# Own order tables for three of four batches, reordered gathers and a rearranged start in a Mamba plus mixture-of-experts kernel

## The chip, the cores and the metric

The kernel runs on one core of a Trainium2 chip. The time is the device time of one execution in microseconds, as the median of several runs. For the kernel before it is 1083.17 us (three runs, 1080.89 to 1084.44).

## The reference

Four sequences of 512 tokens with 512 channels. First a selective scan (Mamba) over a context of 256 channels, gated by the layer-normed x and added to it; then a mixture of 64 experts with the top 6 per token, and a shared expert.

```python
# b = 0..3, L = 512, d_model 256, d_inner 512, d_state 16, dt_rank 16
x1 = einsum('bld,ed->bel', ctx, in_proj_w)
u  = silu(causal_conv4(x1, conv_w) + conv_b)
dt_low, Bm, Cm = split(einsum('bdl,ed->bel', u, x_proj_w), [16, 32], axis=1)
dt = softplus(einsum('brl,dr->bdl', dt_low, dt_proj_w) + dt_proj_b)
A  = -exp(A_log)
state = state * exp(dt * A) + (dt * u) * B      # scan over the 512 steps
y  = sum_n(state * C) + D * u
x  = x + swapaxes(y * silu(layernorm(x)), 1, 2)
h  = layernorm(x)
# 64 experts, hidden 352, top 6 of softmax(h @ gate_w.T), capacity 64 per expert
x  = x + combine(w_down(silu(w_gate h) * w_up h)) + silu(h @ sw_gate) * (h @ sw_up) @ sw_down
```

## The kernel before

All matrices are float32. The work has two phases.

**First phase.** Each of the four batches b has 32 scan steps q (`STEPS`): four blocks of 128 inner channels, times eight pairs of states. A step takes 2 x 512 columns and five operations: `dA` (ScalarE, L918, exp(dt A) into PSUM), `dbu` (GpSimd, L1341, dt u B), `scan` (VectorE, L1105), `weigh` (times C; VectorE at L1112 for odd steps and those in `EXTRA`, GpSimd at L1346 for the others), and `yT` (TensorE, L566, eight transposes that accumulate y in PSUM). The product buffer `R` is a ring of five, so dbu of step q + 5 waits for yT of step q (L1340). `gate` (L1128) and `x2` (L1133) multiply by silu(z) and add x.

Before the scans of a batch stand its preparation: transposes of the context (`ctx`), the projection (`inproj`, L597), the first tap (`acc`, L858), three more taps (`conv`, L1119), `u` (silu), `xdbl` (L605), and, for each block, dt by softplus. The stable softplus is made of ScalarE's exp and ln and four GpSimd operations of 512 columns, `c`, `sp`, `dt` and `dtu` (L1314, L1319, L1323, L1334). After the scans come the layer norm (`xstats` L1155, `xaggr` L1094, `xn` L951, `xnT`), the router (`logits`, `top`, `choose`, `pos`, `places`, `hots`, `ohsid`, `table`) that builds the table of token numbers per expert, and the shared expert of the batch: `sgate` and `sup` (L696, 24 matmuls each, which the trace records as two matmuls apiece), `sdown` (L709, 24 matmuls) and VectorE's addition (L1144). For batch 3 the shared expert's `sup` and `sdown` are done in the second phase.

What each engine does next is fixed by hand-written times. `AT` gives, for each engine and kind of work, the time in steps counted from a batch's first scan, so that 64 + 64.1 for `sdown` of batch 2 is step 128.1, after the last scan; `LAST` overrides it for batch 3. `first_phase` (L339) sorts all of it, and each engine takes its own entries in this order (`mine`). The times decide the order only; semaphores decide when a thing starts. An engine that waits for one entry holds all that are behind it. `BANKS` says which PSUM bank an entry takes.

```python
"dve xstats": [35.07, 35.57, 36.07, 36.23],              # AT
"pe sdown": [64.1, 64.41, 64.47, 65.75, ..., 68.44],     # AT
"dve sdown": [65.41, 67.2, 68.24, 69.79],                # AT
"dve xstats": [34.49, 35.55, 36.17, 36.55],              # LAST, on top of 96
```

**The start.** SyncE issues the context, nine parameter loads that count on one semaphore, then x, zeros and shared weights (L459 to L481). TensorE waits for all nine (L575), transposes all parameters (L576 to L581), waits for their copies (L582), and only then takes its first entry. The buffers of step 0 are cleared and A is made by exp and a sign change.

**Second phase.** 32 pairs q of experts. The weights come in 192 pieces of 704 or 768 KB through 20 slots (`PIECES`, `SLOTS`); the first 20 are fetched around the last scans, each further one when its slot is free (L543). For a pair, GpSimd gathers 128 token rows by an indirect DMA (`gather`, L1355), TensorE transposes them (`tokens`) and does gate and up (`gate_up_mm`, L733), `acts`, `down_mm` (L757) one pair later, and `merge` (L765), which sums rows of a token that is in both experts; GpSimd adds the rows to the output by an indirect DMA (`scatter`, L1365). Each scatter, and each of the four additions of the shared expert of batch 3 (`add_shared`, L1373), waits for the one before it. There are two buffers for gathered rows (`xg`): gather q waits for tokens q - 2 and for VectorE's `weights` q - 2 (L1353). The items of batch 3's shared expert are spread over pairs 0 to 27 (`items`). The orders of the engines around this are:

```python
tokens(0)                                   # TensorE, L792
for q in range(NPAIR):
    if q + 1 < NPAIR: tokens(q + 1)
    gate_up_mm(q)
    if q: down_mm(q - 1)
    acts(q); merge(q - 1); shared items
for q in range(3): gather(q)                # GpSimd, L1381
for q in range(NPAIR):
    if q + 3 < NPAIR: gather(q + 3)
    add_shared items; scatter(q)
```

## Time and profile before

| | |
|---|---|
| median of the runs | 1083.17 us (1080.89 to 1084.44) |
| profiled execution, its own time | 1084.39 us |
| span of the profiled execution | 1082.5 us |
| mean granted TensorE clock | 0.893 |
| busy: TensorE, VectorE, ScalarE, GpSimd | 892.9, 597.4, 503.0, 572.7 us |
| moved by DMA | 250.50 MB, mean 231 GB/s |

The profile is of one execution, taken by the hardware's profiler. PE is TensorE's matmul, PEld its weight load, DVE VectorE, ACT ScalarE, POOL GpSimd, SPq SyncE's queue. L566 is line 566 of the kernel. Times are microseconds from the start of the span. A row of the timeline gives start, duration, engine, line and operation, what it writes and reads, how many instructions it groups (x), and in brackets for how long the engine had been idle and what released it. A row by windows has the busy time of each engine in that stretch with the number of instructions. An engine can be busy and still not be what is waited for.

### The profile page before, as it was taken

What the parts mean: (1) busy time and instruction counts of PE and PEld (TensorE: products, weight loads), DVE (VectorE), ACT (ScalarE), POOL (GpSimd) and SP (SyncE); (2) the same over time, 40 slices, a digit from 0 to 9 for tenths busy, and PEclk for the clock granted to TensorE, in tenths of its full rate; (3) what the DMA queues carried; (4) which work ended last, traced back from release to release, by engine and by line L of the source; (5) the groups of instructions that cost most, each with busy time, mean ns of one, the idle gap of its engine ahead of it and who ended that gap; (6) DMA issues with size and microseconds to landing.
All of it is one profiled execution on the core that took longest, in us unless ns stands there. A gap on an engine that the chain in (4) does not pass through costs nothing.

```text
span 1082.5 us, 12258 instructions
## 1 busy us (share of the span) xinstructions
PE 892.9 (82%) x4049; PEld 482.9 (45%) x4049; DVE 597.4 (55%) x849; ACT 503.0 (46%) x871; POOL 572.7 (53%) x326
## 2 busy tenths in 40 slices
PE   5346745769899778998769998999999899979966
PEld 3144434546454465454645553444444444434432
DVE  2279879998888988898898722212211122111111
ACT  3667653887776778665856333121221112111111
POOL 0398899986988868978877301121122112122211
PEclk9768765588999987999789998999999999998988
DMA  9423434434333434334457391999999999999972
GB/s 330 155 80 115 140 134 145 148 116 161 108 129 134 158 134 146 117 118 145 166 202 260 121 354 38 369 398 395 394 399 398 392 394 400 387 390 399 390 269 30
DMA packets 68361, 250.50 MB, mean 231 GB/s; under 512 B 10522, under 2 KB 13094, under 8 KB 68044
## 3 DMA queue, kind: packets, MB, share of 16 engines
q1 hardware_dynamic: 56332, 226.14, 55.0%
q0 software_dynamic: 7744, 18.88, 7.2%
q10 hardware_dynamic: 4224, 4.72, 1.3%
q8 instruction: 33, 0.54, 0.2%
q14 instruction: 28, 0.23, 0.1%
HBM read 230.54 MB, written 19.17 MB: 231 GB/s over the span
## 4 chain that ended last, share of the span: by engine, by line
PE 53%; DMA 15%; DVE 11%; issue 8%; ACT 6%; POOL 5%; SPq 0%; POOLq 0%; DVEq 0%; ACTq 0%
PE ps L696 12%; PE ps L566 11%; PE ps L733 10%; PE ps L709 6%; DMA out_rows<-xn,idxs 5%; DMA arena<-xn_rows,idu 5%; PE ps L757 5%; DVE ps L1105 4%; DVE arena L1112 3%; PE ps L777 2%; PE ps L765 2%; ACT ps L918 2%; PE ps L597 2%; DMA out_rows<-arena 2%; DMA out_rows<-so_or_scores 2%
## 5 line engine op out<-in xcount | busy, mean ns | idle before, releaser
L566 PE MATMUL ps<-ident,arena 128*128 128x128 f32 (+2 forms) x1408 | 240.6, 326 | 127.5 <-POOL arena L1346 48.1
L1341 POOL TENSOR_TENSOR arena<-arena 128x1024 f32<-128x1024 f32 x128 | 299.8, 2359 | 22.2 <-PE ps L566 12.3
L566 PEld LDWEIGHTS ps<-ident,arena 128*128 128x128 f32 (+2 forms) x1408 | 205.9, 180 | 229.5 <-issue 80.3
L918 ACT ACTIVATE ps<-arena,An 128x511 f32<-128x511 f32 x256 | 165.6, 680 | 104.8 <-DVE ps L1113 79.0
L1105 DVE TENSOR_TENSOR_SCAN ps<-ps,arena 128x1024 f32<-128x1024 f32 x84 | 192.1, 2287 | 19.1 <-POOL arena L1341 9.7
L1365 POOL DMA_INDIRECT out_rows<-xn,idxs x32 | 50.9, 1592 | 278.1 <-ACT xn L817 148.5
L733 PE MATMUL ps<-arena 128*64 128x352 f32 x968 | 165.7, 479 | 0.0
L696 PE MATMUL ps<-xnT,sw 128*128 128x512 f32 (+1 forms) x328 | 154.2, 614 | 3.5 <-ACT arena L881 2.7
L1346 POOL TENSOR_TENSOR arena<-arena 128x1024 f32<-128x1024 f32 x44 | 103.7, 2357 | 53.8 <-DVE arena L1105 53.5
L1245 DVE TENSOR_TENSOR arena<-arena,ps 128x352 f32<-128x352 f32 x32 | 16.7, 521 | 207.5 <-PE ps L733 207.5
L1105 DVE TENSOR_TENSOR_SCAN arena<-ps,arena 128x1024 f32<-128x1024 f32 x44 | 100.4, 2282 | 25.3 <-POOL arena L1341 22.9
L733 PEld LDWEIGHTS ps<-arena 128*64 128x64 f32 x968 | 72.8, 142 | 69.9 <-issue 66.7
L1112 DVE TENSOR_TENSOR arena<-ps,arena 128x1024 f32<-128x1024 f32 x84 | 102.6, 1221 | 2.2
L817 ACT COPY routes<-ps 128x512 f32<-128x512 f32 x32 | 18.7, 585 | 168.2 <-PE ps L745 168.2
L696 PEld LDWEIGHTS ps<-xnT,sw 128*128 128x128 f32 (+1 forms) x328 | 58.4, 189 | 70.2 <-issue 65.5
L757 PE MATMUL ps<-arena,routes 118*64 118x512 f32 (+1 forms) x366 | 88.0, 592 | 0.0
L817 ACT COPY arena<-ps 128x512 f32<-128x512 f32 x60 | 35.0, 585 | 72.7 <-PE ps L566 62.9
L709 PE MATMUL ps<-sw,hs 128*128 128x512 f32 x144 | 67.6, 606 | 0.0
L1252 DVE TENSOR_SCALAR routes<-ps,wcol 128x512 f32<-128x512 f32 x32 | 24.0, 751 | 64.1 <-PE ps L757 64.1
L1355 POOL DMA_INDIRECT arena<-xn_rows,idu x32 | 34.3, 1072 | 34.6 <-DVE idu L1226 10.7
L597 PE MATMUL ps<-arena 128*128 128x512 f32 x64 | 37.2, 722 | 12.8 <-DVE arena L1119 10.8
L1022 ACT ACTIVATE arena<-ps 128x352 f32<-128x352 f32 x32 | 14.8, 464 | 67.7 <-PE ps L733 65.8
(151 smaller groups left out, 942.7 us busy)
## 6 DMA issues: line engine op xcount, KB each, us to landing
arena<-bc_rows SPq DMA_DIRECT2D x128, 512.0 KB, 4.7
arena<-in_L_ffn_w_down SPq DMA_DIRECT2D x60, 768.0 KB, 19.7
arena<-in_L_ffn_w_gate SPq DMA_DIRECT2D x61, 704.0 KB, 20.8
arena<-in_L_ffn_w_up SPq DMA_DIRECT2D x60, 704.0 KB, 16.9
arena<-in_x SPq DMA_DIRECT2D x4, 1024.0 KB, 7.0
xn_rows<-xn ACTq DMA_DIRECT2D x4, 1024.0 KB, 4.3
out_rows<-arena SPq DMA_DIRECT2D x4, 1024.0 KB, 5.0
extra<-in_L_ffn_w_up SPq DMA_DIRECT2D x4, 704.0 KB
```

The lines of the kernel that those rows point to most:

```text
L566: return nc.tensor.matmul(dst, src, ident[0:k, 0:k], is_transpose=True, **kw)
L597: mm = nc.tensor.matmul(ps[:, bank, :], winT[:, m, c * P:(c + 1) * P], ctxT[:, m, :], start=(m == 0), stop=(m == 1))
L696: mm = nc.tensor.matmul(ps[0:m, bank, :], w[:, k, c * P:c * P + m], xnT[:, k, :], start=(k == 0), stop=(k == HC - 1))
L709: mm = nc.tensor.matmul(ps[:, bank, :], hs[0:m, k, c * P:(c + 1) * P], swd[0:m, k, :], start=(k == 0), stop=(k == NI - 1))
L733: mm = nc.tensor.matmul(ps[64 * e:64 * e + 64, 2 + n, 0:I], xgT[q % 2][:, k, 64 * e:64 * e + 64], place(what, q, e)[:, k, :], start=(k == ...
L757: mm = nc.tensor.matmul(ps[64 * e:64 * e + 64, 6 + j, :], hT[j][0:m, k, 64 * e:64 * e + 64], place("down", q, e)[0:m, k, :], start=(k == 0 ...
L817: nc.scalar.copy(dst, src).then_inc(sm, 1)
L918: a = nc.scalar.activation(ps[:, 2 * (c % 2) + n, 1:L], dt[k][:, 1:L], ACT.Exp, scale=An[:, k, NB * g + n:NB * g + n + 1])
L1105: V.tensor_tensor_scan(pair if by_vector(q) else flat(R[q % RING]), pair, flat(R[q % RING]), 0.0, ALU.mult, ALU.add).then_inc(s["scan_done ...
L1112: link(V.tensor_tensor(R[q % RING], ps[:, h:h + 2, :], Crep[n % REPS], ALU.mult))
L1341: G.tensor_tensor(R[c % RING], dtu[k][:, None, :].to_broadcast([P, NB, L]), Brep[n % REPS], ALU.mult)\
L1346: G.tensor_tensor(R[c % RING], R[c % RING], Crep[n % REPS], ALU.mult).then_inc(s["cs_even"], 1)
```

## The change

1. Order tables of their own: `FIRST` for batch 0 and `LATE` for batch 2, beside `AT` (batch 1) and `LAST` (batch 3). Many entries of `AT` and `LAST` shift. `EXTRA` now counts steps over all batches: 8, 3, 4 and 5 even steps of batches 0 to 3 are weighed by VectorE, where it was 5 of each.
2. `c`, `sp`, `dt` and `dtu` of blocks 0 and 1 of batch 0 are done by VectorE (`BYV`).
3. Seven parameter loads go to ScalarE's queue; SyncE issues the context, in_proj_w and gate_w, and waits for all before the large loads. TensorE transposes the identity 14 times (`WARM`), then the context and in_proj_w; VectorE copies in_proj_w; the other parameters are transposed after the second projection matmul group.
4. In batch 3 the second half of `ohsid` (token numbers times the one-hot rows) is done by VectorE.
5. Second phase: `gate_up_mm(q)` goes in front of `tokens(q + 1)`, `silu(q)` in front of `evac_tokens(q + 1)`, and four gathers lead, so that gather q + 4 stands in front of scatter q.

```diff
 AT = {
-    "dve zstats": [-4.93, -4.46, -2.23, -1.03],
+    "dve zstats": [-7.68, -7.21, -4.93, -3.78],
-    "pe sup": [58.22, 58.56, 58.62, 59.14, 59.31, 59.34, 59.41, 60.5, 60.64, 61.24, 61.54, 62.15],
+    "pe sup": [58.66, 59.02, 59.08, 59.6, 59.77, 59.8, 59.87, 60.96, 61.1, 61.7, 62.0, 62.61],
-    "pe sdown": [64.1, 64.41, 64.47, 65.75, 66.2, 66.65, 67.47, 67.69, 67.91, 67.99, 68.14, 68.44],
+    "pe sdown": [64.14, 64.45, 64.51, 64.97, 66.24, 66.69, 67.51, 67.73, 67.95, 68.03, 68.18, 68.48],
...
+FIRST = {
+    "pe ctx": [-28.2, -26.8],
+    "act du": [-11.16, -11.01, 4.51, 5.26],
+    "pool c": [-13.61, -10.93, 2.64, 4.09],
+    "pool sp": [-13.31, -10.76, 3.28, 4.67],
+    "pool dt": [-12.79, -10.73, 3.3, 4.91],
+    "pool dtu": [-11.7, -9.33, 5.24, 5.65],
+    "dve zaggr": [3.72],
...
+LATE = {
+    "dve xstats": [35.07, 35.57, 36.07, 36.3],
+    "act xn": [36.8, 37.2, 37.6, 38.0],
+    "pe xnT": [37.1, 37.7, 38.3, 38.9],
+    "pe sgate": [42.01, 42.51, 43.6, 43.9, 45.87, 46.16, 48.36, 48.52, 48.74, 49.03, 49.41, 49.7],
+    "pe sup": [49.85, 50.25, 50.64, 51.05, 51.27, 51.44, 51.84, 52.24, 52.64, 53.03, 53.99, 54.24],
+    "pe sdown": [56.07, 56.46, 56.86, 57.31, 57.72, 58.1, 58.54, 58.94, 59.35, 59.79, 60.18, 60.58],
+    "dve sdown": [57.55, 58.8, 60.04, 61.27],
...
+FIRSTBANKS = {
+    "ctx": [6, 7],
+    "inproj": [4, 5, 6, 7],
+}
...
 LASTBANKS = {
-    "sgate": [0, 1, 0, 1, 0],
+    "sgate": [0, 1, 0, 3, 0],
-    "sel": [1],
+    "sel": [7],
...
-EXTRA = [4, 6, 12, 22, 24]
+EXTRA = [0, 4, 6, 12, 18, 20, 24, 26, 36, 44, 52, 76, 84, 88, 90, 100, 108, 116, 118, 120]
...
+        def sums_by(b, c):
+            return "dve" if b == 0 and c < BYV else "pool"
+
         def by_vector(q):
-            return q % 2 == 1 or q % STEPS in EXTRA
+            return q % 2 == 1 or q in EXTRA
...
+                    own, own_banks = {0: (FIRST, FIRSTBANKS), B - 2: (LATE, LATEBANKS), B - 1: (LAST, LASTBANKS)}\
+                        .get(b, (AT, BANKS))
...
+        def softplus_sum(engine, E, kind, b, c):
+            i = DC * b + c
+            if i == BYV:
+                engine.wait_ge(s[{"c": "c_ready", "sp": "sum_add", "dt": "dt_ready", "dtu": "dtu_ready"}[kind]], i)
+            if kind == "c":
+                engine.wait_ge(s["wm_ready"], i + 1)
+                E.tensor_tensor(rest[c % 2], ex[c % 2], rest[c % 2], ALU.subtract).then_inc(s["c_ready"], 1)
...
             load(cin, ctx_1024[0].rearrange("(t p) d -> p t d", p=P), s["ctx_in"])
-            load(raw_win, in_proj_w.rearrange("(c p) d -> p c d", p=P), s["par_in"])
+            load(raw_win, in_proj_w.rearrange("(c p) d -> p c d", p=P), s["win_in"])
             load(raw_gw, gate_w, s["par_in"])
+            sp.wait_ge(s["win_in"], 16)
+            sp.wait_ge(s["par_in"], 16 * 8)
...
-            pe.wait_ge(s["par_in"], 16 * 9)
...
-            pe.wait_ge(s["pre_ev"], 6)
+            for n in range(WARM):
+                transpose(ps[:, 5, 0:P], ident[:], start=True, stop=True)
+            def flip_parameters():
+                pe.wait_ge(s["par_in"], 16 * 8)
+                flip(1, 0, [raw_vec]).then_inc(s["pre_t"], 1)
+                flip(3, 0, [raw_xp[:, c * P:(c + 1) * P] for c in range(DC)]).then_inc(s["pre_t"], 1)
+                flip(0, 0, [raw_dtw[:, c, :] for c in range(DC)]).then_inc(s["pre_t"], 1)
+                flip(2, 0, [raw_gw[:, c::HC] for c in range(HC)]).then_inc(s["pre_t"], 1)
...
                     flip(bank, 0, [cin[:, t, c * P:(c + 1) * P] for t in range(LT)]).then_inc(s["ctxT_mm"], 1)
+                    if b == 0 and c == 1:
+                        pe.wait_ge(s["win_in"], 16)
+                        for m in range(2):
+                            flip(m, 0, [raw_win[:, k, m * P:(m + 1) * P] for k in range(DC)]).then_inc(s["pre_t"], 1)
...
                     mm.then_inc(s["inproj_mm"], 1)
+                    if b == 0 and c == 1:
+                        flip_parameters()
...
             for q in range(NPAIR):
+                gate_up_mm(q)
                 if q + 1 < NPAIR:
                     tokens(q + 1)
-                gate_up_mm(q)
...
+            load(raw_xp, x_proj_w, s["par_in"])
...
+                    if i == 0:
+                        act.wait_ge(s["par_in"], 16 * 8)
+                        nc.scalar.activation(An[:], An[:], ACT.Exp).then_inc(s["a_exp"], 1)
+                        nc.scalar.preload_act_table_set("silu_and_others")
+                        act.wait_ge(s["pre_t"], 3)
+                        copy(vec[:], ps[:, 1, 0:3 * DC], s["pre_ev"])
...
-                        nc.scalar.activation(ohsid[:, i % 2, :, n, :], ohs[:, c], ACT.Copy, scale=f)\
-                            .then_inc(s["ohsid_ready"], 1)
+                        if n == 0 or b < B - 1:
+                            nc.scalar.activation(ohsid[:, i % 2, :, n, :], ohs[:, c], ACT.Copy, scale=f)\
+                                .then_inc(s["ohsid_ready"], 1)
...
             for q in range(NPAIR):
+                silu(q)
                 if q + 1 < NPAIR:
                     evac_tokens(q + 1)
-                silu(q)
...
+            for m in range(2):
+                dve.wait_ge(s["pre_t"], m + 1)
+                V.tensor_copy(winT[:, m, :], ps[:, m, :]).then_inc(s["win_ready"], 1)
...
+                elif kind == "ohsid":
+                    dve.wait_ge(s["ohs_ready"], i + 1)
+                    if c >= 2:
+                        dve.wait_ge(s["tab_mm"], i - 1)
+                    with nc.allow_low_precision("whole numbers up to 16, exact"):
+                        V.tensor_scalar(ohsid[:, i % 2, :, 1, :], ohs[:, c], float(i + 1), None, ALU.mult)\
+                            .then_inc(s["ohsid2_ready"], 1)
...
-            for q in range(3):
+            for q in range(4):
                 gather(q)
             for q in range(NPAIR):
-                if q + 3 < NPAIR:
-                    gather(q + 3)
+                if q + 4 < NPAIR:
+                    gather(q + 4)
```

## Rows read from the trace of the kernel before

**Rows 1.** Windows by batch: length; PE, PEld, DVE, ACT, POOL busy; clock, DMA, GB/s

```profile
56.00:187.00 131.00, 74.01 (x315) 55.75 (x316) 113.18 (x99) 79.34 (x125) 122.01 (x61) 0.68 0.37 124
187.00:330.00 143.00, 120.18 (x515) 73.75 (x514) 129.00 (x152) 107.98 (x184) 121.86 (x62) 0.85 0.38 128
330.00:478.00 148.00, 130.53 (x565) 75.56 (x564) 130.90 (x155) 108.42 (x184) 120.34 (x62) 0.93 0.41 140
478.00:611.30 133.30, 112.11 (x513) 67.91 (x512) 117.80 (x135) 85.52 (x151) 104.47 (x51) 0.90 0.51 175
```

**Rows 2.** Chain of waits, the first 23 us: start us, us, what

```profile
4.99 3.29 DMA xnT<-in_L_ffn_gate_w
...
13.26 1.98 PE ps L566 x8
...
15.99 6.52 PE ps L597 x8
```

**Rows 3.** Timeline up to the first scan: start, us, engine, line, what

```profile
19.78 0.78 ACT L858 ACTIVATE arena<-ps,vec,cw 128x512 f32<-128x512 f32 x1 [3.94 <-PE ps L597]
...
43.14 1.26 POOL L1314 TENSOR_TENSOR arena<-arena 128x512 f32<-128x512 f32 x1 [40.14 <-ACT arena L900]
...
49.16 1.28 ACT L918 ACTIVATE ps<-arena,An 128x511 f32<-128x511 f32 x2
...
52.42 1.26 POOL L1334 TENSOR_TENSOR arena<-arena 128x512 f32<-128x512 f32 x1
...
56.10 2.29 DVE L1105 TENSOR_TENSOR_SCAN arena<-ps,arena 128x1024 f32<-128x1024 f32 x1 [22.85 <-POOL arena L1341]
```

**Rows 4.** Timeline from the last scan to the last shared gate products

```profile
608.96 2.29 DVE L1105 TENSOR_TENSOR_SCAN ps<-ps,arena 128x1024 f32<-128x1024 f32 x1
...
612.80 0.68 DVE L1139 TENSOR_TENSOR hs<-hs,ps 64x512 f32<-64x512 f32 x1 [1.55 <-PE ps L696]
...
617.02 20.42 PE L709 MATMUL ps<-sw,hs 128*128 128x512 f32 x44
...
617.95 0.69 DVE L1133 TENSOR_TENSOR arena<-arena,ps 128x512 f32<-128x512 f32 x1
...
633.33 0.38 DVE L1094 BATCH_NORM_AGGREGATE xmv<-xstats 128x2 f32<-128x6 f32 x4
...
648.07 8.75 PE L696 MATMUL ps<-xnT,sw 128*128 128x512 f32 x20
...
661.03 9.99 PE L696 MATMUL ps<-xnT,sw 128*128 128x512 f32 x16 [0.86 <-DVE idu L1226]
```

**Rows 5.** Windows near the end of the expert stage, columns as in rows 1

```profile
1000.00:1040.00 40.00, 38.91 (x192) 17.54 (x188) 8.05 (x26) 8.22 (x15) 9.09 (x7) 1.00 1.03 392
1040.00:1050.00 10.00, 2.05 (x8) 1.26 (x10) 0.22 (x1) 0.58 (x1) 1.58 (x1) 0.61 0.84 254
1050.00:1060.00 10.00, 9.98 (x49) 4.06 (x45) 1.71 (x5) 1.05 (x2) 0.00 (x0) 0.87 0.07 12
```

**Rows 6.** Waits in the expert stage: total us, times, longest us

```profile
PE ps L566 <- DMA arena<-xn_rows,idu: 25.5, 7, 8.9
```

**Rows 7.** Timeline of the last pairs

```profile
1029.56 4.95 PE L733 MATMUL ps<-arena 128*64 128x352 f32 x32
...
1038.59 1.11 POOL L1355 DMA_INDIRECT arena<-xn_rows,idu  x1 [0.30 <-issue]
...
1049.01 6.68 PE L733 MATMUL ps<-arena 128*64 128x352 f32 x32
```

**Rows 8.** Groups by line: count, then busy us and mean ns

```profile
L1346 POOL TENSOR_TENSOR arena<-arena 128x1024 f32<-128x1024 f32 x44 | 103.7, 2357 | 53.8 <-DVE arena L1105 53.5
...
L1112 DVE TENSOR_TENSOR arena<-ps,arena 128x1024 f32<-128x1024 f32 x84 | 102.6, 1221 | 2.2
```

**Rows 9.** A window of batch 3, columns as in rows 1

```profile
520.00:530.00 10.00, 7.18 (x32) 6.55 (x32) 7.38 (x7) 7.60 (x12) 10.00 (x5) 0.50 0.34 107
```

**Rows 10.** DMA issues of the expert stage: count, median us to landing

```profile
out_rows<-xn,idxs POOLq DMA_INDIRECT x32, 8.5
```

More of the change, by code:

```diff
@@ L38 @@
 XBS = 3
+BYV = 2
+WARM = 14
 ASLOTS = 19
@@ L126 @@
[L126 removed]
+    "act scopy": [41.95, 42.1, 47.7, 53.1, 53.56],
+    "dve places": [41.61],
     "pool places": [44.53],
[L128 to L133 removed]
+    "dve hots": [43.32],
+    "act ohsid": [44.97, 45.12, 45.19, 46.45],
+    "pe table": [43.01, 44.15, 45.27, 45.8],
+    "dve table": [47.78],
+    "pe sel": [46.61],
+    "dve ids": [47.79],
```

283 lines of the change are left out of this document (164 added, 119 removed).

## The prediction

> **What bounds the kernel now.** I read the windows by stage first. While the scans of a batch run, no engine is full alone: GpSimd is busy 122.01 of 131 us in batch 0, VectorE 113.18, and in batches 1 and 2 VectorE, TensorE and GpSimd all stand between 120 and 131 us of 143 and 148 [rows 1]. GpSimd is nearest to its limit in batch 0. In batch 3 nothing is full: GpSimd 104.47, VectorE 117.80, TensorE 112.11 of 133.3 us. The chain of waits shows the start: the last of ten loads lands at 8.28, then come all parameter transposes, then the context's, and the first projection matmul runs at 15.99 [rows 2]. The timeline up to the first scan shows GpSimd alone between 43.14 and 53.65: eight 512-column operations of 1.26 us, then the first dbu product, which ends where the scan of 56.10 begins; ScalarE had been ready for its dA at 49.16 [rows 3].
>
> The timeline after the scans is the largest piece. The last scan ends at 611.25, but its weigh starts after a shared-expert product of 612.80, for which VectorE had waited 1.55; then 44 matmul records of the shared down projection of batch 2 hold TensorE for 20.42 us, and the statistics of batch 3, queued on VectorE behind the additions of these products, end only at 633.71 [rows 4]. The gathers can start 27.1 us later, at 660.8 to 661. The expert stage runs with DMA share 1.03 and 392 GB/s until shortly after 1040, then DMA goes quiet [rows 5]; yet the program ends at 1082.5. The waits say why: TensorE waited seven times, 25.5 us, for gathers, 8.9 at the longest [rows 6]. The last gather was issued at 1038.59, behind a scatter; the gate/up block of pair 30 began at 1049.01, when the block before had begun at 1029.56 [rows 7].
>
> **The sum.** It is made against the profiled execution: span 1082.5, its own time 1084.39, so 1.9 lies outside the span; the median shown, 1083.17, is 1.2 below that.
>
> (a) *Start to the first dt sums.* ScalarE issues seven of the parameter loads, SyncE the context, in_proj_w and gate_w first. The projection now needs the first two only, which SyncE issues at the head of the list; the last of today's ten takes 3.29 from issue [rows 2], and with 1 MB ahead I put them at 4 to 5 us. TensorE runs 14 warm transposes, 8 of the context and 8 of in_proj_w; at 1.97/8 = 0.246 us each (the rate of the x8 row) that is 7.4 us from about 2 us (an estimate, GpSimd makes the identity first), to 9.3, plus a copy of about 0.6: first projection at 10.0 instead of 15.99. Two projections (6.52/2 = 3.26, at half clock; half of that if the warm transposes raise it) and the small transpose and copy, 0.7, stand before the first acc: 14 to 17.2, where it was 19.78 [rows 3]. The four convolutions are VectorE's and follow at its pace, 1 us less waiting between them since each projection has a bank. Gain between 3.5 and 7; I take 6, because the transposes run back to back. The seven issues cost ScalarE about 0.45 us each (SyncE's ten took until 4.99, rows 2) while it waits for data anyway; without that cover 3 us. SyncE's new wait for the parameters delays x and the shared weights by about 2 us; their first reader, zstats, now comes after the dt sums, so it costs nothing.
>
> (b) *c, sp, dt, dtu of two blocks on VectorE.* Eight operations leave GpSimd: 10.5 us of chain. No row has VectorE on this shape with both inputs in SBUF; the nearest is x2's 0.69 with one input in PSUM [rows 4], and I take it; the upper bound is GpSimd's 1.26. At 0.69, dt of block 0 is ready soon after ScalarE's ln, dbu starts, and the bound becomes ScalarE: dA issued at 49.16 ends at 50.5 instead of a scan at 56.10, gain 5.6. The four zstats now stand on VectorE before scan 0 (four of about 0.65, an estimate from x2's 0.69, partly in the way): I take 4.5, bounds 2 and 5.6. The Trainium skill (SBUF — State Buffer, "SBUF: two separate sides") says that such a VectorE instruction and a GpSimd one that reads SBUF exclude each other for a whole instruction; by that rule block 1's operations could wait once for a product, 2.4 us, and no trace here shows it.
>
> (c) *Batch 0.* Eight even steps instead of five are weighed by VectorE: GpSimd loses 3 x 2.36 = 7.1, VectorE gains 3 x 1.22 and a small memset each, 3.8 [rows 8]. GpSimd goes to 115, VectorE to 117 of 131. The 9 us that today lie over the fuller engine stay, as they are waits between engines: 126 to 128. I take -4; bounds 0 (the wait was elsewhere) and -7.
>
> (d) *Batches 1 and 2.* Three and four steps instead of five: GpSimd +4.7 and +2.4, VectorE -2.6 and -1.3, towards 127/126 and 123/130 of 143 and 148 [rows 1]. Neither is full; shared-expert entries shift by half a step. 0, bounds -3 and +4 for each.
>
> (e) *Batch 3.* With the table for batch 2 its shared expert begins five steps earlier and its down projection (20.4 us, rows 4) runs inside the scans. TensorE is idle 21 us there, and where it idles it ran at half clock: between 520 and 530 it was 7.18 of 10 us busy at 0.50 [rows 9]. The work fits, with little left over, so a transpose will sometimes be late for the ring of five: +2, bounds -2 and +10.
>
> (f) *Scan end to first gate/up.* Statistics no longer stand behind 44 records. From the scan's end, 611.25, come the weigh 1.22, eight transposes of half of 1.97, gate and x2 of 0.7 each: x2 ends near 615.2 instead of 618.64 [rows 2, 4, 8]; statistics and aggregation, 3 us, end at 618.1 instead of 633.71: -15.6. TensorE's last down group no longer holds the first transpose: -1.1. ohsid on two engines, sgate 3 in its own bank, gate/up 0 ahead of tokens 1: -0.8, -0.9, -0.7; their covers are short. Against it: TensorE is now idle for 7 us before the transposes, and the granted clock falls after such a pause, as [rows 7] show, where 32 records took 6.68 after 8.9 idle, against 4.95: transposes and logits +2, the x20 group in front of the table (8.75, rows 4) +3. Net -13 to -14; I take -13, bounds -8 and -17. Weights are prefetched meanwhile, 3 us earlier than today, and are in by the gathers.
>
> (g) *Expert stage.* Bytes stay, so the end of the weight stream moves only with its start. Past it: gate/up 30 can start at 1029.56 + 9.9 = 1039.5 instead of 1049.01 (-9.5), at full clock (-1.7): -11. Of the other 16.6 us of gather waits, most is hidden today by the saturated DMA; with pair 25 not late the scatter chain, one after another at about 8.5 us landing plus 1 us issue each [rows 10], ends some 3 us sooner. A gather in front costs each scatter up to 1.1 us when it is not waiting anyway. I take -14, bounds -6 and -20.
>
> Sum: -6 -4.5 -4 +0 +2 -13 -14 = -39.5: span 1043, profiled time 1044.9, median 1043.7; forecast **1044**.
>
> **Rivals.** *Weights bound the end* (13%): with gathers early, pair 30 waits for its weights instead, since DMA is saturated until after 1040. For it: share 1.03 throughout. Against: DMA is nearly silent from 1050, while 30 us of program remain. Then (g) gives 3: 1055. *The down projection comes back inside batch 3* (12%): 112 + 20.4 is 132.5 of 133.3 us, and if TensorE's waits (a transpose waits for a weigh) can't be filled, the batch grows by some 17 and not 2: 1059. Against: the idle time lies where the table moves the work. *Better balance* (7%): batches 1 to 3 gain 4 each by their tables: 1032. *The head does not reach the end* (3%): scan 0 comes early but batch 0 is bound by something unseen, and (a) to (c) give 3: 1055. *Slower* (4%): TensorE stays at 1.2 GHz in batch 3. The 144 records of batch 2's shared expert cost 0.44 to 0.46 us at full clock and about 0.81 at half [rows 2, 4]; in the 20 steps that the table gives them that is 117 us and not 64, with the transposes of these steps +20 more. It adds about 60 us beyond (e) and ends near 1104. It decides from a mean clock of about 0.65 there. Against: wherever TensorE is continuously busy, as in the 20.42 us group, the granted clock was full.
>
> **How the numbers follow.** Forecast 61%, rivals 13, 12, 7, 3 and 4. My case's own range is 1030 to 1056; to leave out no more than 2 in 10 over all cases the range is 1030 to 1062. About 0.3% (3 us) can be told from no change. All cases but the slow one lie beyond it; I keep 2% for terms that cancel, and 5% slower.
>
> **What would show it.** First projection near 10 us; scan 0 near 45.6; scan 32 near 172; no down-projection records after the last scan; ids about 25 us before today's 660.8; no wait of TensorE for gathers over 3 us; gate/up 30 about 10 us after gate/up 29; fewer than 28 us from gate/up 30 to the end. Wrong would be: TensorE full with GpSimd and VectorE waiting for it in batch 3, or long waits on weights at the end.

## The result, and the profile after

The kernel after the change takes 1055.62 us (median of four runs, 1054.00 to 1056.89), against 1083.71 us (1080.89 to 1084.44) before: a ratio of 0.9738 [0.9712, 0.9764], 28 us faster. The forecast was 1044, range 1030 to 1062. The profiled execution has a span of 1053.9 us (1082.5 before) and a mean granted clock of 0.889.

Cut at the starts of scans 0, 32, 64, 96 and 127 and of the first gate/up block, the two spans compare like this (us):

| stage | before | after | difference | forecast |
|---|---|---|---|---|
| start to scan 0 | 56.1 | 46.1 | -10.0 | -10.5 (a, b) |
| batch 0 | 131.0 | 126.8 | -4.2 | -4 (c) |
| batch 1 | 142.6 | 146.0 | +3.4 | 0 (d) |
| batch 2 | 148.2 | 150.0 | +1.8 | 0 (d) |
| batch 3, to its last scan | 131.1 | 142.1 | +11.0 | +2 (e) |
| last scan to gate/up 0 | 65.0 | 50.1 | -14.9 | -13 (f) |
| gate/up 0 to the end | 408.6 | 392.8 | -15.8 | -14 (g) |

Six of the seven stages lie within 3.5 us of the forecast; batch 3 misses it by 9. The windows by stage of the kernel after (columns as in [rows 1]; the last scan ends at 613.30) show what it is full of:

```profile
46.10:172.94 126.84, 77.57 (x315) 57.03 (x316) 117.43 (x110) 83.01 (x135) 112.98 (x58) 0.63 0.38 131
172.94:318.90 145.96, 119.18 (x514) 73.89 (x513) 125.91 (x148) 111.34 (x186) 126.84 (x64) 0.83 0.38 129
318.90:468.90 150.00, 132.19 (x565) 76.70 (x564) 129.75 (x154) 111.41 (x186) 122.77 (x62) 0.92 0.39 138
468.90:613.30 144.40, 130.63 (x571) 72.29 (x569) 120.86 (x136) 80.17 (x140) 103.48 (x50) 0.97 0.46 158
550.00:600.00 50.00, 50.00 (x183) 25.34 (x182) 39.27 (x37) 21.61 (x32) 30.14 (x13) 1.00 0.61 206
550.00:581.30 31.30, 31.30 (x115) 15.68 (x114) 23.94 (x25) 15.84 (x23) 16.27 (x8) 1.00 0.56 193
```

Against [rows 1], GpSimd went from 122.0 to 113.0 us in batch 0, and TensorE from 112.1 to 130.6 in batch 3. Between 550 and 600 us TensorE is busy for all of 50.00 us at full clock, while VectorE and GpSimd have 11 and 20 us of idle time: for that stretch TensorE is the bound. The waits of batch 3 (engine, line, releaser: total us, times, longest us) are:

```profile
ACT ps L1043 <- DVE ps L1242: 33.2, 11, 6.0
...
POOL arena L1466 <- PE ps L664: 18.4, 8, 3.7
...
DVE arena L1285 <- PE ps L825: 9.3, 6, 3.0
```

The first is ScalarE, which waits for VectorE. The other two are waits for TensorE. L1466 is `dbu`, L664 the transposes of `yT`: the ring of five product buffers is not emptied in time. Before, this wait had been 1.0 us in the same batch. L1285 is VectorE's addition of a down projection (L825), and 5.8 of its 9.3 us of waiting fall behind 590 us, where batch 2's own runs. The timeline shows one turn of the wait for the ring:

```profile
565.90 5.32 PE L812 MATMUL ps<-xnT,sw 128*128 128x512 f32 x12
566.24 2.35 POOL L1466 TENSOR_TENSOR arena<-arena 128x1024 f32<-128x1024 f32 x1 [3.67 <-PE ps L664]
...
571.05 1.04 PE L664 MATMUL ps<-ident,arena 128*128 128x128 f32 x8
571.93 3.60 PE L812 MATMUL ps<-xnT,sw 128*128 128x512 f32 x8
572.26 2.36 POOL L1466 TENSOR_TENSOR arena<-arena 128x1024 f32<-128x1024 f32 x1 [3.68 <-PE ps L664]
```

Twelve shared-expert matmuls (5.32 us) stand in front of eight transposes, and GpSimd starts its next product 0.17 us after the transposes' last modelled end.

The starts of the scans say where in batch 3 the 11 us arise. Scan 114 comes 76.9 us after scan 96 before and 81.3 after, which is 4.4 us more. From there to scan 120 it takes 26.0 and 31.1 us, 5.2 more, and from scan 120 to 127 it takes 28.2 and 29.7, 1.5 more. The down projection of batch 2 begins only behind scan 120 (581.30):

```profile
581.71 1.88 PE L825 MATMUL ps<-sw,hs 128*128 128x512 f32 x4
```

So 9.5 of the 11 us are there before its first matmul. They arise while the table runs the shared expert's gate and up products, earlier and closer together than before. From scan 114 to 120 TensorE is busy for all of the time (550.00:581.30 above); in the kernel before it had room in these steps:

```profile
555.00:581.00 26.00, 19.08 (x91) 11.91 (x90) 22.43 (x21) 11.92 (x22) 17.93 (x10) 0.80 0.56 212
```

**The start.** These are the steps of (a) and (b) in the timeline after; L701 is the projection, L543 to L555 the softplus sums, L1291 `zstats`, L1234 the scan:

```profile
1.87 3.17 PE L664 MATMUL ps<-ident 128*128 128x128 f32 x14 [1.87 <-POOL ident L1438]
...
8.86 3.67 PE L701 MATMUL ps<-arena 128*128 128x512 f32 x8 [1.04 <-DVE arena L1215]
...
37.96 0.69 DVE L555 TENSOR_TENSOR arena<-arena 128x512 f32<-128x512 f32 x1
...
38.73 2.35 POOL L1466 TENSOR_TENSOR arena<-arena 128x1024 f32<-128x1024 f32 x1 [35.73 <-DVE arena L555]
...
40.14 1.49 DVE L543 TENSOR_TENSOR arena<-arena 128x512 f32<-128x512 f32 x1 [1.49 <-ACT arena L1023]
...
43.72 2.47 DVE L1291 BATCH_NORM_STATS2 zstats<-arena 128x6 f32<-128x512 f32 x4
...
46.11 2.28 DVE L1234 TENSOR_TENSOR_SCAN ps<-ps,arena 128x1024 f32<-128x1024 f32 x1
```

The projection takes 3.67 us for eight records where it took 6.52 [rows 2]: it now runs at full clock. Scan 0 starts where `zstats` ends. Its product had ended at 41.08 and ScalarE's exponentials of the first two steps at 44.42, so at that point VectorE's own queue, and no data, holds it.

**The tail of the first phase** (L1221 is `xaggr`, L758 the logits, L812 `sgate`, L1480 the gather):

```profile
611.02 2.27 DVE L1234 TENSOR_TENSOR_SCAN ps<-ps,arena 128x1024 f32<-128x1024 f32 x1
...
613.57 3.68 PE L664 MATMUL ps<-ident,arena 128*128 128x128 f32 x16 [3.50 <-POOL arena L1471]
...
621.32 0.38 DVE L1221 BATCH_NORM_AGGREGATE xmv<-xstats 128x2 f32<-128x6 f32 x4
...
624.38 1.96 PE L664 MATMUL ps<-ident,xn 128*128 128x128 f32 x8 [7.13 <-ACT xn L1076]
...
629.70 5.22 PE L758 MATMUL ps<-gwT,xnT 128*128 128x64 f32 x24
...
640.61 8.75 PE L812 MATMUL ps<-xnT,sw 128*128 128x512 f32 x20
...
653.59 1.27 POOL L1480 DMA_INDIRECT arena<-xn_rows,idu  x1 [9.82 <-DVE idu L1367]
```

No down projection stands behind the last scan any more, and the statistics end 10.7 us after its start instead of 24.8 [rows 4]. TensorE idles 3.50 and 7.13 us, and what follows each pause runs at half speed: sixteen transposes in 3.68 us, where sixteen took 1.97 just before, at 608.11. The windows of the same stretch give the granted clock (behind the busy times), for these transposes, the logits and the group of 20:

```profile
613.60:617.20 3.60, 3.60 (x16) 3.25 (x16) 2.40 (x4) 0.00 (x0) 0.00 (x0) 0.50 1.01 417
629.70:634.70 5.00, 5.00 (x25) 5.00 (x25) 0.00 (x0) 0.59 (x1) 0.00 (x0) 0.50 1.01 390
641.00:649.00 8.00, 8.00 (x20) 3.52 (x19) 6.08 (x21) 2.19 (x4) 0.46 (x2) 1.00 0.42 159
```

The group of 20 takes 8.75 us, as in [rows 4], at the full clock.

**The end.** The list of waits of the expert stage has no wait of TensorE for gathers left, where it was 25.5 us [rows 6]. The chain that ended last, for its last 75 us (only its DMA steps are shown; start us, us, what):

```profile
980.46 8.45 DMA out_rows<-arena
...
989.79 8.33 DMA out_rows<-xn,idxs
...
999.00 8.99 DMA out_rows<-xn,idxs
...
1008.53 7.80 DMA out_rows<-so_or_scores
...
1017.21 8.28 DMA out_rows<-xn,idxs
...
1026.37 9.63 DMA out_rows<-xn,idxs
...
1036.86 4.72 DMA out_rows<-xn,idxs
...
1042.44 4.70 DMA out_rows<-xn,idxs
```

From 980 us on, the end is set by additions to the output that wait for one another, about 9.4 us from one start to the next while the weights still stream and 5.6 after. The gathers are no longer in it.

### The profile page after: what moved, and what is told of

Same layout as the page of the kernel before. It is cut to its first block, busy times and chain, and to the rows that moved or that the text cites. A ratio compares the mean times of both kernels' runs of the same rounds, so it can differ in the third digit from the quotient of the medians.

```text
span 1053.9 us, 12293 instructions
## 1 busy us (share of the span) xinstructions
PE 896.8 (85%) x4063; PEld 481.7 (46%) x4063; DVE 604.6 (57%) x863; ACT 503.7 (48%) x867; POOL 562.3 (53%) x318
## 4 chain that ended last, share of the span: by engine, by line
PE 56%; DVE 14%; DMA 12%; ACT 8%; issue 8%; POOL 2%; POOLq 0%; SPq 0%; DVEq 0%; ACTq 0%
PE ps L812 13%; PE ps L664 13%; PE ps L849 11%; DMA out_rows<-xn,idxs 7%; PE ps L873 6%; DVE ps L1234 5%; PE ps L825 4%; DVE arena L1241 3%; PE ps L881 2%; PE ps L893 2%; DVE arena L1260 2%; ACT ps L1043 2%; DMA out_rows<-arena 2%; DMA out_rows<-so_or_scores 2%; DMA arena<-bc_rows 1%
## 5 line engine op out<-in xcount | busy, mean ns | idle before, releaser
L1466 POOL TENSOR_TENSOR arena<-arena 128x1024 f32<-128x1024 f32 x128 | 299.7, 2357 | 73.0 <-DVE arena L555 38.5
L664 PE MATMUL ps<-ident,arena 128*128 128x128 f32 (+2 forms) x1408 | 244.0, 327 | 95.2 <-POOL arena L1471 25.1
L664 PEld LDWEIGHTS ps<-ident,arena 128*128 128x128 f32 (+2 forms) x1408 | 204.3, 180 | 201.5 <-issue 84.6
L1234 DVE TENSOR_TENSOR_SCAN ps<-ps,arena 128x1024 f32<-128x1024 f32 x84 | 192.1, 2287 | 17.0 <-ACT ps L1043 16.0
L812 PE MATMUL ps<-xnT,sw 128*128 128x512 f32 (+1 forms) x328 | 157.6, 624 | 12.2 <-ACT arena L1004 10.5
L849 PE MATMUL ps<-arena 128*64 128x352 f32 x968 | 160.0, 462 | 0.8 <-ACT arena L933 0.8
L1480 POOL DMA_INDIRECT arena<-xn_rows,idu x32 | 34.2, 1069 | 218.1 <-DVE wcol L1379 133.5
L1234 DVE TENSOR_TENSOR_SCAN arena<-ps,arena 128x1024 f32<-128x1024 f32 x44 | 100.5, 2284 | 2.5 <-ACT ps L1043 2.5
L1490 POOL DMA_INDIRECT out_rows<-xn,idxs x32 | 50.8, 1589 | 94.2 <-DVE idxs L1406 40.1
L812 PEld LDWEIGHTS ps<-xnT,sw 128*128 128x128 f32 (+1 forms) x328 | 59.1, 192 | 78.1 <-issue 64.7
L825 PE MATMUL ps<-sw,hs 128*128 128x512 f32 x144 | 68.6, 606 | 0.0
L1406 DVE SCALAR_TENSOR_TENSOR idxs<-dup,moff,idf 128x1 uint32<-128x1 f32 x32 | 7.0, 219 | 66.2 <-DMA out_rows<-xn,idxs 65.6
```

Of the source, the lines that this page charges most:

```text
L664: return nc.tensor.matmul(dst, src, ident[0:k, 0:k], is_transpose=True, **kw)
L812: mm = nc.tensor.matmul(ps[0:m, bank, :], w[:, k, c * P:c * P + m], xnT[:, k, :], start=(k == 0), stop=(k == HC - 1))
L825: mm = nc.tensor.matmul(ps[:, bank, :], hs[0:m, k, c * P:(c + 1) * P], swd[0:m, k, :], start=(k == 0), stop=(k == NI - 1))
L849: mm = nc.tensor.matmul(ps[64 * e:64 * e + 64, 2 + n, 0:I], xgT[q % 2][:, k, 64 * e:64 * e + 64], place(what, q, e)[:, k, :], start=(k == ...
L1234: V.tensor_tensor_scan(pair if by_vector(q) else flat(R[q % RING]), pair, flat(R[q % RING]), 0.0, ALU.mult, ALU.add).then_inc(s["scan_done ...
L1466: G.tensor_tensor(R[c % RING], dtu[k][:, None, :].to_broadcast([P, NB, L]), Brep[n % REPS], ALU.mult)\
```

## The experiments

All kernels start from the kernel after; line numbers are its own unless said otherwise. Each time is a median of four to six runs, compared with the kernel before on the same chip (1084.39, 1084.59 and 1084.72 us in the three sets). The kernel after was not run again in these sets; its ratio rests on its own four runs. The stages come from one trace each, and their spread differs. The code of batch 0 is the same in eight of the kernels beside the kernel after, and their spans of it are 124.2 to 126.9 us; batch 1, with the same code in ten, takes 144.2 to 149.3. So in these two a difference of 3 and of 5 us between two single traces means nothing. Batch 3 is steadier: 141.9 to 142.2 us in the seven traces with the same tables and `EXTRA`.

### The expert stage: three kernels

**Old order of TensorE and ScalarE, gathers in front.**

```diff
-                gate_up_mm(q)
                 if q + 1 < NPAIR:
                     tokens(q + 1)
+                gate_up_mm(q)
```

(and the same for `silu(q)` and `evac_tokens(q + 1)`)

> The changed kernel, with tokens(q + 1) back in front of gate_up_mm(q) (and ScalarE's copy in front of its silu), the gathers still four ahead. The trace after shows a pair period of 10.27 us where it was 9.91, because tokens stand between gate/up and down. Theory A: it is the early gathers that give the gain of the expert stage, the extra 0.36 us of 31 pairs is partly hidden by the saturated DMA: 1050 to 1056, periods back at 9.91, no long wait for a gather. Theory B: the order of TensorE is what gives the gain, because a late gather then finds work in front of it: 1062 to 1070.

Measured: 1057.26 us (1052.50 to 1059.74), ratio 0.9740 [0.9714, 0.9765]; gate/up 0 to the end 394.9 us. The signs are those of theory A (a pair takes 9.91 us, and TensorE does not wait for a gather); the time is 1.3 us above its range.

**New order, three gathers in front as before.**

```diff
-            for q in range(4):
+            for q in range(3):
                 gather(q)
             for q in range(NPAIR):
-                if q + 4 < NPAIR:
-                    gather(q + 4)
+                if q + 3 < NPAIR:
+                    gather(q + 3)
```

> The changed kernel with three leading gathers as before, TensorE's new order kept. Theory A (the gathers give it): waits for gathers come back, less the 4.9 us that gate/up now stands in front of tokens; the last gather is issued behind a scatter again: 1059 to 1066. Theory B (TensorE's order gives it): 1055 to 1058.

Measured: 1053.69 us (1049.72 to 1057.44), 0.9712 [0.9685, 0.9739]; stage 394.1 us; TensorE waits for gathers 1.3 us in all. Theory A is refuted, and the time is 1.3 us below theory B's range.

**Both undone.**

> The changed kernel with the expert stage wholly as before. From gate/up 0 to the end the stage took 408.6 us before and 392.8 after. If the two halves add up to that: 1055.6 + 15.8, 1069 to 1073. If part of the 15.8 came from the stage starting in another phase against its prefetch: 1060 to 1067.

Measured: 1070.99 us (1069.45 to 1072.54), 0.9870 [0.9851, 0.9889]; stage 407.9 us, as before the change (408.6).

Both together are worth 15 us, and either of them alone gives all of it, within the intervals. The waits of TensorE in the expert stage say what it meets instead. First with both undone, then with only the order undone:

```profile
PE ps L664 <- DMA arena<-xn_rows,idu: 24.7, 6, 9.0
```

```profile
PE ps L873 <- DMA arena<-in_L_ffn_w_down: 14.3, 7, 3.7
```

Once no gather is late, the stage runs into the weights (with the old order or the old gathers) or into the chain of additions (with both new), and all three kernels end 393 to 395 us after gate/up 0. The chain that ended last has a transfer of down weights in it in the kernels with one half undone (24.1 and 24.9 us), and the additions in the kernel after. The new order of TensorE has a price of its own. With it a pair takes 10.27 us, or 13.71 with shared-expert matmuls in it (gate/up blocks at 701.90, 712.17, 725.88 in the kernel after), and with the old one 9.91 and 13.35 (from 704.58 to 714.49 and from 727.13 to 740.48 before): 0.36 us a pair more. In the chains of these two kernels, near 980 us, the four transposes take 0.68 us with the new order for 0.47 with the old one, and the twelve down products 2.73 for 2.58. With transposes between gate/up and down, TensorE changes once more a pair between 64-column and 128-column weights; that this is the reason is argued, not shown. The price is hidden: the stage is as long with the new order as with the old one.

### Batch 2's own table

**Batch 2 by `AT`, without `LATE`.**

```diff
-                    own, own_banks = {0: (FIRST, FIRSTBANKS), B - 2: (LATE, LATEBANKS), B - 1: (LAST, LASTBANKS)}\
+                    own, own_banks = {0: (FIRST, FIRSTBANKS), B - 1: (LAST, LASTBANKS)}\
```

> The changed kernel with batch 2 by the common table, so that its down projection stands after the last scan again. Theory A: batch 3 grew by 11 us because this work fills TensorE there; without it batch 3 shrinks to 133 to 136 us, the statistics end some 12 us later against the last scan, TensorE keeps its full clock after them, and the time is 1053 to 1060, so the own table is worth little. Theory B: batch 3 grew by the other shifts (EXTRA, the tables); it stays at 142 to 146 and the time rises to 1065 to 1070.

Measured: 1054.46 us (1053.31 to 1056.16), 0.9719 [0.9703, 0.9734]: no slower than the kernel after. Batch 3 to its last scan takes 131.7 us instead of 142.1, and the last scan to gate/up 0 takes 59.2 instead of 50.1. Its timeline (L825 is `sdown`) shows the down projection behind the last scan, as before, and full clock afterwards:

```profile
601.19 2.29 DVE L1234 TENSOR_TENSOR_SCAN ps<-ps,arena 128x1024 f32<-128x1024 f32 x1
...
608.82 20.42 PE L825 MATMUL ps<-sw,hs 128*128 128x512 f32 x44
625.13 0.38 DVE L1221 BATCH_NORM_AGGREGATE xmv<-xstats 128x2 f32<-128x6 f32 x4
...
632.60 2.79 PE L758 MATMUL ps<-gwT,xnT 128*128 128x64 f32 x24
```

The wait of `dbu` for `yT` in its batch 3 is 5.6 us instead of 18.4. So the 9 us that the prediction missed are this table's, and it gives 9 in the tail and takes 10 in batch 3. Here too the difference is there before the down projection: scan 120 comes 101.7 us after scan 96 instead of 112.4. Which entries of the table cost it was not tried.

**The last column group of batch 2's down projection (12 of 48 matmuls, as recorded) behind the last scan.**

```diff
-    "pe sdown": [..., 59.35, 59.79, 60.18, 60.58],
-    "dve sdown": [57.55, 58.8, 60.04, 61.27],
+    "pe sdown": [..., 59.35, 65.0, 65.1, 65.2],
+    "dve sdown": [57.55, 58.8, 60.04, 69.3],
```

(and the output row's store later, `"sp out"` from 62.71 to 71.0)

> The changed kernel with the last of four column groups of batch 2's down projection (12 records, 5.7 us) moved behind the last scan, where TensorE is idle for 7.1 us before the first transposes; its addition stands behind the statistics and the store of batch 2 behind the prefetches. If batch 3 is bound by TensorE: it shrinks by 4 to 6 us to 138 to 140, the transposes and logits run at full clock and save another 3 to 5, time 1045 to 1049. If the growth of batch 3 has another cause: batch 3 stays at 144, only the clock helps, 1051 to 1054.

Measured: 1052.63 us (1048.25 to 1055.82), 0.9707 [0.9674, 0.9739]. Batch 3 139.3 us, so 2.8 less, and the tail 49.9, unchanged: the group lies in time that was idle, though it does not keep the clock. The timeline has the pause in front of the last transposes of `yT` as before, and behind them the group, which takes 6.24 us for 12 records:

```profile
606.31 3.67 PE L664 MATMUL ps<-ident,arena 128*128 128x128 f32 x16 [3.59 <-POOL arena L1471]
609.78 6.24 PE L825 MATMUL ps<-sw,hs 128*128 128x512 f32 x12
```

The windows have the group mostly at full clock and the logits at half again, though TensorE had been idle for only 1.09 us between the group and the transposes in front of them:

```profile
609.80:616.10 6.30, 6.22 (x13) 2.28 (x12) 4.28 (x11) 1.54 (x7) 0.00 (x0) 0.89 0.64 190
622.40:627.40 5.00, 5.00 (x26) 5.00 (x25) 0.00 (x0) 0.60 (x2) 0.00 (x0) 0.50 1.02 397
```

So the first theory's 1045 to 1049 was missed: batch 3 shrank by less than 4 to 6 us, and the 3 to 5 us of the clock did not come.

**Identity transposes in the two pauses of the tail**, 20 in front of the last `yT` entries and 24 in front of `xnT`:

```diff
...
                 elif kind == "xnT":
+                    if i == DC * (B - 1):
+                        claim(3)
+                        for n in range(24):
+                            transpose(ps[:, 3, 0:P], ident[:], start=True, stop=True)
                     claim(bank)
```

> The changed kernel with 20 transposes of the identity in front of the yT of step 126 and 24 in front of the first transpose of batch 3, where TensorE is idle for 3.5 and 7.1 us; nothing else. In the trace after, the 16 transposes behind the first pause took 3.68 us (1.97 at full clock) and from the end of the statistics to gate/up 0 went 39.4 us, 35.2 in the kernel whose down projection keeps TensorE busy there. If the half clock is what costs: 1.7 + 4.2, time 1049 to 1052. If not, or if the transposes are in the way: 1054 to 1058.

Measured: 1050.83 us (1047.95 to 1052.41), 0.9681 [0.9658, 0.9703]. In its timeline (its lines are 8 higher from L758 on) the sixteen transposes take 2.25 instead of 3.68 us, and the logits 3.28 instead of 5.22:

```profile
612.32 2.25 PE L664 MATMUL ps<-ident,arena 128*128 128x128 f32 x16 [1.32 <-POOL arena L1479]
614.40 2.78 PE L664 MATMUL ps<-ident 128*128 128x128 f32 x24
618.81 0.38 DVE L1229 BATCH_NORM_AGGREGATE xmv<-xstats 128x2 f32<-128x6 f32 x4
...
627.19 3.28 PE L766 MATMUL ps<-gwT,xnT 128*128 128x64 f32 x24
```

The tail is 45.7 us instead of 50.1. Of these 4.4 us only part is sure to come from the edit: two kernels without it (the old `EXTRA` and the old `AT`, below) also had their logits in 3.32 and 3.62 us in the profiled execution and a tail of 46.9, while seven had 5.22. What is the edit's alone is the first sixteen transposes: in the nine kernels that have them behind a pause of 3.50 to 3.59 us with nothing in it, they took 3.32 to 3.68 us.

**Both together**, with 6 and 12 identity transposes, and one third of the last group still inside the scans (`"pe sdown"` ending 59.35, 63.2, 65.0, 65.1).

> The changed kernel with the last column group of batch 2's down projection at 63.2, 65.0 and 65.1 steps (one third before the last two yT, two behind them), with 6 and 12 transposes of the identity to fill up. The split alone gave 3 us (1052.6), with the last yT and the transposes still at half clock. If both effects add: 1045 to 1049. If they are the same microseconds: 1050 to 1053.

Measured: 1047.95 us (1044.36 to 1048.57), 0.9656 [0.9633, 0.9678], span 1043.4. Batch 3 139.4, tail 45.2. The gains of the two add up: 3.0 and 4.8 us against the kernel after, and 7.7 together. With the intervals of these ratios, each about 5 us wide or more, the sum is not known better than to some microseconds.

**The groups before it spread as well** (`"pe sdown"` ending 57.72, 58.54, 59.35, 60.3, 61.2, 62.2, 63.2, 65.0, 65.1; `"dve sdown"` 57.55, 59.6, 62.8, 69.3).

> As the kernel before it, with groups 1 and 2 of the down projection also spread out, to 57.7 to 62.2 steps, so that one matmul pair follows each yT. If batch 3 is long because TensorE's groups make yT late for the ring of five buffers in steps 114 to 124: GpSimd's waits on yT (18.4 us, 8 times) shrink and batch 3 gets 2 to 4 us shorter than in that kernel, 1043 to 1047. If TensorE's total is what counts: no difference between the two.

Measured: 1047.22 us (1045.74 to 1049.69), 0.9657 [0.9636, 0.9678]. Batch 3 is down to 137.4 us, but in the profiled execution the logits took 5.22 us again and the tail 48.6, so that the time is the same as of the kernel above. Between 550 and 600 TensorE is still 49.44 of 50 us busy.

Batch 3 is 2.0 us shorter, at the edge of the first theory's range, but not for its reason: GpSimd's wait for `yT` is what it was, 18.4 us in 8 times, here and in the two kernels with a split before it (18.3 and 18.4). Of these 18.4 us, 14.6 lie between 557 and 582 us in the kernel after, beside the gate and up products, which none of these edits moves. What shrank is VectorE's wait for the down projection, from 9.3 us over 7.2 to 5.4. So the ring's wait belongs to the gate and up products, and how much of the batch's growth it makes was not tried.

### The start, and batch 0

**The sums on GpSimd again** (`BYV = 0`; the clearing of the PSUM columns of step 0 then stands in front of `zstats`).

> The changed kernel with c, sp, dt and dtu of batch 0 on GpSimd again. Theory A: eight operations of 1.26 in place of 0.69 us stand between ScalarE and the first product, and block 1's stand in front of scan 1; scan 0 moves from 46.1 to 50 to 52, GpSimd has more in front of it, and batch 0 does not make it good: time +4 to +8 on the changed kernel's 1055.6. Theory B: batch 0 is bound by VectorE once it weighs eight even steps, and GpSimd catches up: scan 0 moves, scan 32 moves by under 2 us, time within 2 of 1055.6.

Measured: 1061.22 us (1057.26 to 1062.39), 0.9783 [0.9756, 0.9811]. Its timeline again has the chain of eight operations of GpSimd, of which the first and the last are shown, and scan 0 2.29 us later than in the kernel after:

```profile
35.42 1.27 POOL L543 TENSOR_TENSOR arena<-arena 128x512 f32<-128x512 f32 x1 [32.42 <-ACT arena L1023]
...
44.70 1.26 POOL L555 TENSOR_TENSOR arena<-arena 128x512 f32<-128x512 f32 x1
45.92 4.64 POOL L1469 TENSOR_TENSOR arena<-arena 128x1024 f32<-128x1024 f32 x2
48.40 2.30 DVE L1234 TENSOR_TENSOR_SCAN ps<-ps,arena 128x1024 f32<-128x1024 f32 x1 [22.88 <-POOL arena L1469]
```

Batch 0 is 126.8 us in both: what the sums give stays. The trace shows 2.3 us of it; the medians differ by 5.6, and the rest has no place in the trace, which is of the second fastest of the six runs. Scan 0 did not move to 50 or later, as theory A had it: here the product of step 0 is what it waits for, and in the kernel after it is `zstats`.

**No warm transposes** (`WARM = 0`).

> The changed kernel without the 14 transposes of the identity at the start. In the trace after, the 16 transposes of context and in_proj_w took 1.05 and 1.09 us per eight and the 8 records of the first projections 3.67; before it was 1.97 per eight and 6.52. If the 14 transposes are what raised the clock: 1.9 + 2.9 us come back in front of the first acc, scan 0 at 50 to 51, time +3 to +5. If TensorE reaches full clock anyway by then: scan 0 at 46 to 47, no change.

Measured: 1056.46 us (1055.09 to 1058.72), 0.9750 [0.9725, 0.9776]: no difference that can be told, where 3 to 5 us were expected. The trace has the half clock at the head, with 1.94 and 1.97 us for the eight transposes that took 1.05 and 1.09, the projection at 10.03 instead of 8.86, and scan 0 at 48.84, 2.7 later. Batch 0 is 124.9 us, and scan 32 comes 0.8 later: what the head loses is not seen at scan 32. Whether batch 0 gave it back or happened to be a short one can't be told, since 124.2 to 126.9 is its spread.

**Five even steps of each batch on VectorE, as before.**

```diff
-EXTRA = [0, 4, 6, 12, 18, 20, 24, 26, 36, 44, 52, 76, 84, 88, 90, 100, 108, 116, 118, 120]
+EXTRA = [32 * b + n for b in range(4) for n in (4, 6, 12, 22, 24)]
```

> The changed kernel with five even steps of every batch weighed by VectorE. Theory A: the new split gives batch 0 its 4 us and takes 3.4 and 1.8 from batches 1 and 2; then batch 0 is 130 to 132, batch 1 142 to 144, batch 2 148 to 149, and the time 1053 to 1057. Theory B: batches 1 and 2 grew by the shifted tables: they stay at 146 and 150 and the time rises by 4 to 1059 to 1061.

Measured: 1057.14 us (1055.86 to 1059.59), 0.9754 [0.9728, 0.9779]. Batch 0 is 129.6 us, 2.8 more than in the kernel after and above the spread; batches 1 to 3 are 146.2, 150.3 and 144.0. So the even steps explain the gain of batch 0, and not the growth of batches 1 and 2. The last scan starts 5.5 us later than in the kernel after, and the profiled execution makes most of it good behind it: the tail is 46.9 us for 50.1, with the logits at full clock for the most part (3.32 us), and the expert stage 390.8 for 392.8.

**`AT` and `BANKS` of the kernel before**, with `FIRST`, `LATE`, `LAST` and `EXTRA` of the kernel after on top.

> The changed kernel with the common table AT and its banks as they were (own tables of batches 0, 2 and 3, EXTRA and STEP stay new). Batches 1 and 2 took 142.6 and 148.2 us before and 146.0 and 150.0 after, and stayed there with the old EXTRA. If AT's shifts cost it: 142 to 144 and 148, time 1050 to 1053. If the cost is in STEP or in TensorE's clock: 145 to 146 and 150, time 1054 to 1058.

Measured: 1050.45 us (1047.22 to 1052.40), 0.9678 [0.9656, 0.9701], 5 us faster than the kernel after, and the intervals don't meet. Batch 2 takes 146.3 us, while it is 147.7 to 150.3 in all kernels with the new `AT`; batch 1 takes 144.5, inside their 144.2 to 149.3. But batch 3, whose table lies on top of `AT`, takes 145.1, 3.0 more than in the kernel after, and the last scan starts at 609.6 us, where it starts at 608.9 to 612.0 in six kernels with the new `AT`. What the trace has beside that is a tail of 46.9 us for 50.1, with a clock that had come back as in the kernel with the old `EXTRA`. So the old `AT` gives 3.7 us in batch 2 and costs 3.0 in batch 3; the 5 us of the medians have no place in the trace, which is of the slowest of the five runs. That the shifts of `AT` are a loss is not shown.

## Why the prediction was right, and where it was not

The measured time is inside the range and on the forecast side, 11.6 us above the forecast; by stages, -28.7 us stand where -39.5 were forecast. Of the signs named, the projection, scans 0 and 32, the gathers and the missing down projection came about. The ids came 8.3 us before the old 660.8 and not 25, and one of the signs of being wrong is there too: TensorE full in batch 3, with GpSimd and VectorE waiting for it.

- **(a) and (b), the head, -10.0 for -10.5.** Right as a sum, by a different split. The first projection started at 8.86 and not 10.0, because the context and in_proj_w transposes took 1.05 and 1.09 us and not 1.97 each: the warm transposes had raised the clock. `acc` came at 12.93, a gain of 6.85 where I took 6 of at most 7. Seven of the eight sums cost 0.69 us, as taken, and one 1.49, but they gave 2.3 us in the trace and not 4.5. The cause named as "partly in the way" was all in the way: `zstats`, 2.47 us, ends where scan 0 begins.
- **(c), batch 0, -4.2 for -4.** Right, and put on `EXTRA` by an experiment (2.8 of it); the rest is inside the spread.
- **(d), batches 1 and 2, +5.2 for 0.** Each batch lies inside its bound of +4, but both lean the same way. "Shared-expert entries shift by half a step" was passed over without a price. The old `AT` gave 3.7 us back in batch 2 and took 3.0 in batch 3, so what the shifts cost stays open.
- **(e), batch 3, +11.0 for +2. This is the step that failed.** The mechanism was named and the term mis-sized. "The work fits, with little left over" compared 132.5 us of work with 133.3 us of batch as if any idle time of TensorE could take it. The table puts the work into the last 100 us of the batch: TensorE is full from 550 to 600 us, and its idle time stands before (10.5 us between 490 and 550) and after (3.2 us). Nor is it the down projection's 20.4 us that lengthen the batch where they run: 9.5 of the 11 us arise before them, with the gate and up products that the table moves up to make room, and 1.5 beside them. That the down projection runs inside the scans was right; what it displaces had no term. The windows of the kernel before show where the room was: TensorE was idle 21 us between 498 and 578 (6.9 of them between 555 and 581), but busy for all of the 33.3 us from 578 to the last scan's end, where the table puts the down projection. So the gate and up products that stood there had to go into the 80 us before. The bound of +10 was nearly the value, and the rival beside it had 17 from the same two numbers; what came was between them. Taking the table out returned batch 3 to 131.7 us. The late transposes "for the ring of five" did come, 18.4 us of waits, but that they are what the batch grew by is not shown.
- **(f), -14.9 for -13.** The way from the last scan to the statistics became 14.1 us shorter, for 15.6. Of the clock's price, transposes and logits cost more than 2: 1.7 on the sixteen transposes, 2.4 on the logits (5.22 against 2.79 without the table), 1.8 on the first shared products (3.73 against 1.94). The +3 on the group of 20 was wrong: it took 8.75 us, and the granted clock was full again from 639.7 us, before it began. The small edits around the table (ids on two engines, bank 3, gate/up 0 first) gave more than the 2.4 that I took: without `LATE`, statistics to gate/up 0 is 34.8 us, where it was 40.2. The order of gate/up 0 is as taken, 0.7: with the old order the tail is 50.8 us for 50.1. So are the ids: from the start of the group of 20 to their end it takes 12.1 us for 12.9. The banks gave 3.8 and not 0.9: the last sixteen gate products waited for the ids and took 9.99 us [rows 4], and now take 7.13 us from 651.80, 0.9 ahead of the ids' end. So the sum came out near by luck: what the banks gave more, the clock took.
- **(g), -15.8 for -14.** Right in size, and by luck in part. Gate/up 30 starts 354.4 us after gate/up 0 instead of 375.1, a gain of 20.6, and from it to the end it takes 38.3 us, where under 28 was the sign and 33.5 the old value, because the chain of additions now holds the end. Not seen: that either half of the change alone would give it. The rival that the weights bound the end did not come about here; in the two kernels that undo one half TensorE does wait for weights, and they too end as early, so its price (a gain of 3 only) was wrong. The chain of additions, which bounds the kernel itself, I had as a side term of 3 us to be gained.

Of the rivals, the one that the down projection comes back inside batch 3 came about by half (+11 in batch 3, not +17), and the gain of the table was thereby cancelled: with it and without it the kernel takes the same time. The slower rival did not occur: the clock in batch 3 was 0.97. Its price was added up wrongly as well: 117 for 64 us and 20 more make 73 and not 60. The head did reach the end of batch 0: scan 32 comes 14.2 us earlier, for 14.5. Balance did not help batches 1 to 3.

The best versions measured are the change with the last group split and the pauses filled: 1047 to 1048 us, 0.9656 [0.9633, 0.9678], 8 us under the kernel after. Not tried are the old `AT` under it, and `LATE` with the gate and up products where `AT` has them.

## What to carry to other kernels

Before work is moved under another stage, look at the idle time of its engine in windows of the length of the moved piece, and not at the sum over the stage: over batch 3 TensorE had 21 us to spare, and with the work moved in it had none left in 50 us of it. Ask also what has to move away for it: here 9.5 of the 11 us arose with that, before the moved piece began. When a late transfer is taken out of a saturated stage by two means, try each alone, because the next bound (here the weights, then the chain of additions) is often so near that one is enough. And what takes an engine out of the end of a stage also takes its clock: price the short chain behind it at both levels.

## What the runs showed of the hardware

- The additions to the output, each of which the kernel makes wait for the one before, take 7.8 to 9.6 us while the weights stream (1000 to 1030 us: DMA share 1.03), and the last two 4.7 us afterwards.
- After 3.50 and 7.13 us of idle TensorE the granted clock was 0.50, its lower level (1.2 GHz), for what followed. In the kernel after it stayed there from 612.4 to 639.7 us, through the second pause, the 24 logits and four shared products. In two kernels (the old `EXTRA` and the old `AT`) it rose before the second pause, fell in it and rose again during the logits: they took 3.32 and 3.62 us, and 5.22 in seven others. With few identity transposes in the pause (12) it came out either way, and in the kernel with the last group split the logits took 5.22 us behind an idle time of only 1.09 us.
- An operation of VectorE with both inputs in SBUF took 1.49 us instead of 0.69 at 40.14, while GpSimd's product ran from 38.73 to 41.08; it ended 0.55 us behind the product's end. The Trainium skill (SBUF — State Buffer, "SBUF: two separate sides") lets such a pair exclude each other for a whole instruction; by that rule the operation starts at 41.08 and ends near 41.77, and it ended at 41.63, so the trace agrees. It is one such case in eight operations and costs 0.8 us. It comes about in each of the twelve traces that have these sums on VectorE: there the operation lasts from 1.49 to 2.65 us, by how early it meets the product, and in all twelve it ends 0.55 us behind the product's end.
- The transposes of the next tokens between gate/up and down, instead of ahead of both, cost TensorE 0.36 us a pair: 10.27 for 9.91 us, and nothing else of the pair differs.
